# An audio-tower layer on one core: ScalarE's bulk transfers, half of the q and k products, and the token scatters placed in other slots of a hand-written schedule

## The reference

```
h  = concat(x[t], x[t+3], x[t+6]) @ W.T + b           # 744 tokens per sequence
h += Attn(layernorm(h))      # 16 heads of 16, causal, then Wp and bp
h += MoE(layernorm(h))       # 4 experts, top 2, 256 -> 1024 -> 256, exact gelu
MoE: out = sum over the 2 picks of gate * (y_e - c_e + sum of all c)
```

## Time and profile before

| | |
|---|---|
| median of 3 runs | 2007.22 us (2000.09 to 2011.86) |
| the profiled execution | 1999.6 us, of which its span is 1997.9 us |
| batches in the span (first exponential of each) | 134.1, 269.6, 414.0, 561.9, 705.9, 851.7, 997.6, 1145.1 us; the last exponential starts at 1256.9 |
| busy in the whole span | PE 79%, DVE 56%, POOL 42%, ACT 36% |
| mean granted TensorE clock | 0.877 of full speed |

### The profile page before, as it was taken

How to read it: one execution, slowest core, us unless ns; L and a number is a source line. 1 busy time by engine, 2 the same in 40 slices (tenths; PEclk the granted TensorE clock), 3 DMA queues, 4 the chain that set the end, 5 groups by cost and what they waited for, 6 DMA issues and landing times. The chain is left out here.

```text
span 1997.9 us, 33531 instructions
## 1 busy us (share of the span) xinstructions
PE 1582.5 (79%) x10648; PEld 1202.1 (60%) x10648; DVE 1120.3 (56%) x3458; ACT 715.2 (36%) x1463; POOL 832.2 (42%) x912
## 2 busy tenths in 40 slices
PE   2578697697697796797697687309999999999997
PEld 2446364364364374374274342209999999999997
DVE  1266467567567576576577473204555555555554
ACT  0114344344344443443444354102333333333332
POOL 4313234444443534534535425231445444544454
PEclk9769788798698798798898697659999999999999
DMA  3351533733743733724625533157554555555552
GB/s 94 69 91 55 134 83 91 171 84 83 163 98 88 164 79 105 165 60 134 140 58 141 122 87 87 35 182 236 185 189 155 182 192 176 168 184 185 168 178 70
DMA packets 190014, 256.27 MB, mean 128 GB/s; under 512 B 35092, under 2 KB 127182, under 8 KB 189840
## 3 DMA queue, kind: packets, MB, share of 16 engines
q1 hardware_dynamic: 132144, 167.22, 31.3%
q10 hardware_dynamic: 34080, 49.79, 8.3%
q0 software_dynamic: 23616, 37.12, 6.3%
HBM read 173.92 MB, written 75.29 MB: 125 GB/s over the span
## 5 line engine op out<-in xcount | busy, mean ns | idle before, releaser
L593 ACT ACTIVATE prob<-stb 124x496 f32<-124x496 f32 (+2 forms) x832 | 402.8, 504 | 569.8 <-PE stb L963 423.8
L724 DVE CUSTOM_DVE_ANT_0 unused<-mxb,mask_row 124x372 bf16<-124x372 f32 (+4 forms) x768 | 354.2, 484 | 174.9 <-PE mxb L946 169.7
L946 PE MATMUL mxb<-kst,qst 96*124 96x372 bf16 (+4 forms) x1024 | 343.5, 368 | 133.8 <-DVE mxp L724 91.8
L963 PE MATMUL stb<-qst,kst 99*124 99x372 bf16 (+4 forms) x1024 | 319.6, 346 | 110.8 <-ACT prob L593 104.9
L1359 PE MATMUL yb<-w2p,hp 128*128 x2448 | 339.8, 284 | 13.0 <-DVE yo L1299 13.0
L1346 PE MATMUL l1b<-x2T,w1s 128*128 128x384 f32 x1632 | 339.1, 344 | 1.2 <-DVE x2T L1258 1.2
L946 PEld LDWEIGHTS mxb<-kst,qst 96*124 96x124 bf16 x1024 | 139.7, 148 | 332.4 <-DVE mxp L724 169.0
L1359 PEld LDWEIGHTS yb<-w2p,hp 128*128 128x128 f32 x2448 | 323.6, 189 | 23.5 <-issue 23.5
L1196 ACT ACTIVATE hf<-l1b,b1c 128x384 f32<-128x384 f32 x272 | 158.0, 581 | 355.1 <-PE l1b L1346 350.8
L539 POOL TENSOR_SCALAR_AFFINE_SELECT prob<-prob 124x496 f32<-124x496 f32 x192 | 118.0, 623 | 389.4 <-ACT prob L593 389.1
L1346 PEld LDWEIGHTS l1b<-x2T,w1s 128*128 128x128 f32 x1632 | 277.4, 190 | 1.6 <-DVE x2T L1258 1.6
(11 more groups left out here) (158 smaller groups left out, 1565.9 us busy)
## 6 DMA issues: line engine op xcount, KB each, us to landing
w1s<-ws SPq DMA_DIRECT2D x34, 2048.0 KB, 8.4
qk_s<-parts SPq DMA_DIRECT2D x192, 93.0 KB
kst<-qk_s SPq DMA_DIRECT2D x192, 93.0 KB, 4.1
xg<-xs SPq DMA_DIRECT2D x34, 396.0 KB, 3.2
qst<-qk_s SPq DMA_DIRECT2D x32, 279.0 KB, 5.6
wraw<-in_w_all ACTq DMA_DIRECT2D x32, 256.0 KB
ws<-whi ACTq DMA_DIRECT2D x32, 256.0 KB
ws<-wlo ACTq DMA_DIRECT2D x32, 256.0 KB
```

Source lines behind the costliest of these rows:

```text
L593: act.activation(dst, src, ACT.Exp, scale=DH ** -0.5).then_inc(exp_done, 1)
L724: done = dve.tensor_tensor_reduce(out=unused[:, n % 2, e * w:(e + 1) * w], in0=src, in1=mask_row[:, T - w:T], scale=1.0, scalar=-3.0e38, o ...
L946: done = nc.tensor.matmul(out, qst[g % NG][0:ROWS, h + e, TT * i:TT * i + TT], kst[g % NG][0:ROWS, h + e, k0:k0 + w], start=True, stop=True)
L963: done = nc.tensor.matmul(out, kst[g][:, h, TT * j:TT * j + TT], qst[g][:, h, q0:q0 + w], start=True, stop=True)
```

## The change

Only `body_events` changes. In the order of the list:

- wstore 0 to 3 from slots 19, 39, 59, 79 to 17, 34, 63, 85; wsplit 1 to 3 from 31, 51, 71 to 28, 57, 76; wload 2 and 3 from 42 and 62 to 47 and 66.
- h1_store from 43 to 53, res_load from 78 to 73, x_load from 98 to 97. h2_store stays at 41.
- load_stack 0 from 54 to 51; qk 4 to 7 from 50, 53, 56, 59 to 59, 62, 65, 68.
- count and place from 57, 58, 59 to 54, 55, 56; scatters from 61 to 99 to 58 to 95.

```diff
-        put(57, "count", 0)
-        put(58, "place", 0)
-        put(59, "place", 1)
-        for i, s in enumerate((61, 64, 67, 71, 74, 77, 81, 84, 88, 91, 95, 99)):
+        put(54, "count", 0)
+        put(55, "place", 0)
+        put(56, "place", 1)
+        for i, s in enumerate((58, 61, 64, 67, 71, 74, 78, 81, 84, 88, 91, 95)):
             put(s, "scatter", i)
...
-    for n, s in enumerate((2, 22, 42, 62)):
-        put(s, "wload", n)
-        put(s + 9, "wsplit", n)
-        put(s + 17, "wstore", n)
-    put(78, "res_load", 0)
+    for n, (load, split, store) in enumerate(((2, 11, 17), (22, 28, 34), (47, 57, 63), (66, 76, 85))):
+        put(load, "wload", n)
+        put(split, "wsplit", n)
+        put(store, "wstore", n)
+    put(73, "res_load", 0)
...
-        put(43, "h1_store", 0)
+        put(53, "h1_store", 0)
         for n in range(4):
             put(38 + 3 * n, "qk", n)
-            put(50 + 3 * n, "qk", n + 4)
-        put(54, "load_stack", 0)
+            put(59 + 3 * n, "qk", n + 4)
+        put(51, "load_stack", 0)
         put(72, "load_stack", 1)
         put(83, "load_stack", 2)
-        put(98, "x_load", 1)
+        put(97, "x_load", 1)
```

## The result

The changed kernel takes 2017.75 us (median of 18 runs, 2010.62 to 2027.42), the kernel before beside it 2004.05 (18 runs, 1988.56 to 2013.97). The ratio is **1.0074, 95% interval 1.0052 to 1.0096**: slower by 0.7%, where 1929 was forecast. The profiled execution is 2016.5 us, of which the span is 2014.8.

What follows compares the result with a forecast made beforehand. The bound: ACT held at a DMA issued too soon behind a 750 KB one. Savings of 10.2 us in batches 1 to 6, 3.6 in batch 0 and 13 in batch 7, together 78, gave a 1929 us median; range 1874 to 1982.

Steps and rivals of the forecast that it cites:

- What bounded the kernel before: Slots 42 and 79: a DMA too soon behind a 750 KB one holds ACT 6 to 13 us; PE waits 104.9.
- The bulk transfers: Slots 43 and 81: spaced from ACT's next DMA, large transfers stop blocking: -3.61 us in seven batches, -9.42 in eight.
- Products 4 to 7: Slot 58: moved to slots 59 to 68, they no longer wait for product 3's stores: -3.0 us in six batches.
- Stack 0 three slots earlier: Stack load on SP: not waited for in batch 4, and SP gains three slots; zero.
- the second rival: Slot 66: stack 0 lands late beside the h1 store, 4 us in seven batches; 1957, 1982 with upper bounds; chance 0.18.
- The order on SP and the wait at slot 98: Slot 98: SP's later stores delay the inverses' spread; PE waits 8.2 us for POOL's mask, 5.8 more than before.
- A rule against this change: h1 store, slots 53 to 63: at 60 KB/us over four DMA engines it lasts 13 us, stack 0 issued into it.
- Rival 3: Slot 63: ACT's block behind the h1 store only moves, PE losing 5 us; 17 us slower, 2024; chance 0.07.

Runs made afterwards that it cites:

- b_split: Kernel before with ScalarE's three 124-partition transfers (h1, res, out) each issued as two, of 112 and 12 partitions: 1886.40 us, ratio 0.9419.
- b_qk59: Kernel before with only products 4 to 7 moved to slots 59 to 68 and load_stack 0 to slot 51: 2000.42 us, ratio 0.9988.
- a_split: Changed kernel with ScalarE's three 124-partition transfers (h1, res, out) each issued as two, of 112 and 12 partitions: 1907.40 us, ratio 0.9552.
- a_split62: Changed kernel with ScalarE's three 124-partition transfers each issued as two halves of 62 partitions: 2146.54 us, ratio 1.0709.
- a_split_res78: a_split with the load of res back in slot 78 instead of 73: 1905.15 us, ratio 0.9517 to the kernel before.
- a_h1_98: Changed kernel, unsplit, with the store of h1 in slot 98 instead of 53: 2003.33 us, ratio 1.0006 to the kernel before.

## Why the prediction was wrong, step by step

- **What bounded the kernel before**: right. ACT was held at the issue behind a large transfer, and b_split took PE's row from 104.9 to 7.3 us by making those transfers short.
- **The bulk transfers, -3.61 in seven batches and -9.42 in eight**: as waits for ACT, right: 104.9 us became 2.5. As time at slot 43 it was wrong. I let the store of `out` leave the sum once ACT was no longer held; it still delayed the stores of product 0, and PE lost 3.8 to 5.1 us at slot 49 in six batches instead.
- **Products 4 to 7, -3.0 in six batches**: right in size (20 us in b_qk59), and given back at stack 0 (12 us) and `negp` (8 us). The later stores on SP I had booked at 2.0 us of issue time only. The part by itself: 0.9988.
- **"Stack 0 three slots earlier ... Zero"**: this is the step that failed. I asked whether the stack load would pass the h1 store, and not what must land first. Its stores, those of product 3, are issued 0.33 us behind h1 and are read back. They let stack 0 go after 11.5 us; with no h1 store beside them it is 4.2. I had priced this in the second rival at 4 us a batch, 28 in all. It was 8 to 12, 73 us more than before. The rival's two sums also do not follow one working. 1957 charges the 28 us in full beside an unchanged wait at slot 98, and 1982 is the 7.5 us in seven batches on 1929 with none of the 28; with both it is 2010.
- **negp**: not in the sum at all, 48 us. I followed `res` only to the inverses, which are two steps behind it on SP, and not to the three small DMAs issued in the same microsecond, nor did I ask what SP's late coming costs them.
- **The order on SP and the wait at slot 98**: the chain was right and its terms close: landing of the inverses 11.3 us (7.9 taken, bound 11.5), spread 9.5 (9 taken), PE's wait 5.7 in batch 3 (8.2 worked out). Over the run the row is 32.7 us where the working makes about 57, so this term was too dear and hid part of the error.
- **A rule against this change**: I had the rate, 57 to 60 KB/us, and the rule, and gave them a chance of 0.18 and a place in a rival. The times, rates and shares of a_split and a_split62 follow them. The mean granted clock did not rise when ACT's stalls went and others came (0.877 before, 0.870 after); in b_split, where PE's waits fell by 80 us together, it did (0.908).
- **Rival 3**, on whose side the result lies, is not what happened: no issue of ACT at slot 63 or 85 took over 2.1 us. The mechanism for slower was rival 2's, at two to three times its price, with `negp` beside it.

The error under all of it: I treated the block of ACT as the cost of the large transfers. It was one sign of it. That the stalls had been shelter, in which SP's queue caught up, is my reading and not shown by a run of its own.

## What to carry to other kernels

Before moving a long transfer away from an engine that it blocks, list every small transfer that is issued within its duration at the new place, and follow each to who waits for its landing; a queue's MB in a stretch gives the duration. Better, first look at why it is long. Here a transfer of 124 partitions ran at 19.5% of the 16 DMA engines, and cutting it into 112 and 12 was worth 5.8%, with no event moved. When a block disappears and the time does not fall, sum the waits by releaser before and after; the new rows name the place.

## What the runs showed of the hardware that I had not expected

- A 124-partition transfer ran at 57 KB/us, two of 62 at 35, one of 112 with one of 12 at 245, with the same rows of about 1 KB.
- A DMA behind such a transfer held the issuing engine up to 14 us, even where the two were halves of one copy (13.96 us for the pair in a_split62), while the same pair as 112 and 12 took 0.94 us for h1.
- The three 6 KB `negp` transfers, issued beside the load of `res`, let PE go only 8.9 us after the last of them was issued (679.52 + 2.33 to 690.73). Beside the split, short load of a_split it was still 7.3 to 9.9 us; with `res` behind them, in a_split_res78, it was 4.9 (620.17 + 3.01 to 628.06).
- Three 93 KB stores beside a 124-partition store let their reader go 10.7 to 13.9 us behind the first issue, and 4.1 to 4.2 us with none beside them (seven batches each, changed kernel and a_h1_98).
